# Single-row fetches of a graph kernel: one 1,024-byte piece per row, or sixteen 64-byte pieces, at other rates per queue

## What is computed

```python
w_ij  = silu(ef1 @ W1r + b1r) @ W2r + b2r + silu(ef2 @ W1s + b1s) @ W2s + b2s   # per edge, 128 values
q_i   = (x @ Wq)[dst]; k_j = (x @ Wk)[src]; v_j = (x @ Wv)[src]                 # gathered per edge
alpha = (q_i * w_ij * k_j).sum over each head of 16, / 4, * edge_weight          # 8 heads
out   = segment_sum(alpha * v_j, dst) / 16
y     = layernorm(x + out)
```

## Time and profile before

| | |
|---|---|
| median of 3 runs | 3112.95 us |
| lowest, highest | 3109.12 us, 3114.18 us |
| span of the profiled execution, first to last instruction | 1968.8 us |
| what lies around the span (median less span) | 1144.2 us |
| PE busy | 1721.6 us, 87% of the span |
| VectorE busy | 1571.4 us, 80% |
| GpSimd busy | 1486.6 us, 76% |
| ScalarE busy | 580.1 us, 29% |

### The profile page before, as it was taken

The page is one execution under the profiler, slowest core; times in us unless marked ns, Lnnn a source line. Parts: engine busy times, 40 slices in busy tenths (PEclk is TensorE's granted clock), DMA queues, the critical chain, the costliest instruction groups (busy, mean ns, idle before and its releaser), DMA issues.

```text
span 1968.8 us, 57037 instructions
## 1 busy us (share of the span) xinstructions
PE 1721.6 (87%) x14511; PEld 1255.5 (64%) x14511; DVE 1571.4 (80%) x4327; ACT 580.1 (29%) x1031; POOL 1486.6 (76%) x1568
## 2 busy tenths in 40 slices
PE   8799999999998988888888888888888888888898
PEld 7566666666666666666666656666656565656666
DVE  5588888888887887787777878778777778777887
ACT  5332233333322322232222322222222222222223
POOL 7777777777777777777777777777777777777777
PEclk9899999999998999899888999899999989998988
DMA  9866656666666556555555555555556555565654
GB/s 340 257 173 173 176 173 175 174 175 169 168 169 172 162 167 174 153 172 163 166 154 171 164 166 170 156 173 155 173 156 172 161 166 167 162 172 156 174 154 116
DMA packets 191285, 339.03 MB, mean 172 GB/s; under 512 B 83101, under 2 KB 101262, under 8 KB 190958
## 3 DMA queue, kind: packets, MB, share of 16 engines
q0 software_dynamic: 74192, 202.08, 35.9%
q1 hardware_dynamic: 107696, 126.28, 21.6%
q10 hardware_dynamic: 9070, 7.02, 1.4%
HBM read 320.25 MB, written 14.95 MB: 170 GB/s over the span
## 4 chain that ended last, share of the span: by engine, by line
POOL 51%; PE 25%; issue 18%; DVE 3%; DMA 2%; DVEq 0%; ACT 0%; ACTq 0%; SPq 0%
POOL kvt L672 51%; PE bank L710 11%; PE bank L687 4%; PE bank L725 2%; PE bank L712 2%; DMA kvt<-kvtab,srcS 2%; PE bank L750 1%; PE bank L315 1%; PE bank L700 1%; DVE t L994 1%; PE bank L441 1%; DVE accT L948 1%; PE bank L429 1%; DMA qtab<-qx 0%; PE bank L419 0%
## 5 line engine op out<-in xcount | busy, mean ns | idle before, releaser
L672 POOL DMA_INDIRECT kvt<-kvtab,srcS x1527 | 1449.2, 949 | 465.9 <-issue 461.0
L796 ACT ACTIVATE hs<-bank,B 128x512 f32<-128x512 f32 x806 | 509.4, 683 | 1350.8 <-issue 783.4
L710 PE MATMUL bank<-W2r,hs 128*128 128x128 f32 x3224 | 494.8, 300 | 8.7 <-ACT hs L796 8.7
L994 DVE TENSOR_TENSOR t<-bank,kvt 128x512 f32<-128x512 f32 (+1 forms) x395 | 264.9, 671 | 292.8 <-DMA kvt<-kvtab,srcS 158.0
L710 PEld LDWEIGHTS bank<-W2r,hs 128*128 128x128 f32 x3224 | 419.2, 203 | 86.2 <-issue 71.8
L710 PE MATMUL bank<-W2s,hs 128*128 128x128 f32 x3224 | 453.3, 287 | 0.0
L710 PEld LDWEIGHTS bank<-W2s,hs 128*128 128x128 f32 x3224 | 421.3, 204 | 0.0
L725 PE MATMUL bank<-msg,oh 128*32 128x128 f32 x3216 | 177.4, 292 | 221.5 <-DVE accT L948 218.8
L725 PEld LDWEIGHTS bank<-msg,oh 128*32 128x32 f32 x3216 | 71.7, 109 | 411.8 <-issue 395.9
L1009 DVE TENSOR_REDUCE bank<-t 128x32 f32<-128x512 f32 x402 | 279.3, 695 | 13.8
L687 PE MATMUL bank<-eft,W 32*128 32x512 f32 x1612 | 279.2, 669 | 2.4 <-ACT kvh L481 2.4
(11 more groups left out here) (112 smaller groups left out, 704.5 us busy)
## 6 DMA issues: line engine op xcount, KB each, us to landing
kvA<-kvtab ACTq DMA_DIRECT2D x3968, 1.0 KB
kvS<-kvtab SPq DMA_DIRECT2D x3328, 1.0 KB
eft<-in_ef SPq DMA_DIRECT2D x102, 512.0 KB, 7.4
dbt<-dst SPq DMA_DIRECT2D x102, 384.0 KB, 6.7
kvt<-kvtab,srcS POOLq DMA_INDIRECT x1527
qwt<-qtab SPq DMA_DIRECT2D x403, 24.0 KB
kvtab<-kvt SPq DMA_DIRECT2D x24, 256.0 KB, 7.7
qtab<-qx SPq DMA_DIRECT2D x12, 384.0 KB, 6.4
```

What stands on the lines that cost most here:

```text
L672: pool.indirect_dma_start(kvt[:, (g - HX) % KS, t, :], None, kvtab, bass.IndirectOffsetOnAxis(ap=srcS[:, g * TG + t:g * TG + t + 1], axis= ...
L710: pe.matmul(WB[g % 2][:, t * D:(t + 1) * D], hs[:, g % HS, j, t * 128:(t + 1) * 128], w2[:, :], start=(j == 0 and t == 0), stop=False, ski ...
L796: act.activation(hs[:, g % HS, j, :], HB[i % 4][:, :], ACT.Silu, bias=B1[:, j:j + 1]).then_inc(m_si, 1)
L994: m = dve.tensor_tensor(t1[:, s, a:b, :], tiles(WB[s][:, :])[:, a:b, :], kv[:, :, 0:D], ALU.mult)
```

## The change

Three things change. The rates become 10 rows a group on SyncE and 11 on ScalarE, throughout. A row is written by its DMA not as 1,024 contiguous bytes but as 16 pieces of 64 bytes; piece a of buffer 0 and piece a of buffer 1 lie side by side in the partition, so the pieces of one row are 128 bytes apart. VectorE reads the tile in that layout: a piece is one head of 16 float32 values, 8 pieces are the 128 values of k and the other 8 those of v. The number of DMAs for a row stays one.

```diff
-RS, RA = (8, 9, 272), (10, 10, 0)
+RS, RA = (10, 10, 0), (11, 11, 0)
+PIECES = 16
...
-        kvS = sb("kvS", [128, 2, 2 * D], f32)
-        kvA = sb("kvA", [128, 2, 2 * D], f32)
+        kvS = sb("kvS", [128, PIECES, 2, 2 * D // PIECES], f32)
+        kvA = sb("kvA", [128, PIECES, 2, 2 * D // PIECES], f32)
...
-                return kv_bytes[bass.ds(start_of(reg, (N - 1) * KVROW), KVROW)].rearrange("(o f) -> o f", o=1)
+                return kv_bytes[bass.ds(start_of(reg, (N - 1) * KVROW), KVROW)].rearrange("(o a f) -> o a f", o=1, a=PIECES)
...
-                        sp.dma_start(kvS[p:p + 1, u % 2, :].bitcast(u8), kv_row(sp_row[r - rows_upto(g // BS * BS, RS)])
+                        sp.dma_start(kvS[p:p + 1, :, u % 2, :].bitcast(u8), kv_row(sp_row[r - rows_upto(g // BS * BS, RS)])
...
-                        act.dma_start(kvA[p:p + 1, u % 2, :].bitcast(u8), kv_row(act_row[r - rows_upto(g // BA * BA, RA)])
+                        act.dma_start(kvA[p:p + 1, :, u % 2, :].bitcast(u8), kv_row(act_row[r - rows_upto(g // BA * BA, RA)])
...
+            def heads(t):
+                return t.rearrange("p (h d) -> p h d", h=H)
+
+            def row_tile(g, k):
+                buffer, u = (kvS, use_s[g] % 2) if g in use_s else (kvA, use_a[g] % 2)
+                half = buffer[:, k * PIECES // 2:(k + 1) * PIECES // 2, u, :]
+                return half if PIECES == 2 * H else half.rearrange("p a (h d) -> p (a h) d", d=HD)
...
-                for a, b, kv in kv_parts(g):
-                    m = dve.tensor_tensor(t1[:, s, a:b, :], tiles(WB[s][:, :])[:, a:b, :], kv[:, :, 0:D], ALU.mult)
+                n = gathered(g)
+                m = dve.tensor_tensor(t1[:, s, 0:n, :], tiles(WB[s][:, :])[:, 0:n, :], kv_rows(g)[:, 0:n, 0:D], ALU.mult)
+                if n == KT:
+                    m = dve.tensor_tensor(heads(t1[:, s, KT, :]), heads(tiles(WB[s][:, :])[:, KT, :]), row_tile(g, 0),
+                                          ALU.mult)
...
+                if n == KT:
+                    m = dve.tensor_tensor(heads(msg[:, g % MS, KT, :]), row_tile(g, 1),
+                                          cut_alpha(g)[:, KT * H:TG * H].rearrange("p (h a) -> p h a", a=1)
+                                          .broadcast_to([128, H, HD]), ALU.mult)
```

More of the change, by code:

```diff
@@ L1025, in gnn_program @@
                 dve.wait_ge(m_al, g + 1)
[L1026 to L1030, removed]
+                m = dve.tensor_tensor(msg[:, g % MS, 0:n, :].rearrange("p t (h d) -> p t h d", h=H),
+                                      kv_rows(g)[:, 0:n, D:2 * D].rearrange("p t (h d) -> p t h d", h=H),
+                                      cut_alpha(g)[:, 0:n * H].rearrange("p (t h a) -> p t h a", h=H, a=1)
+                                      .broadcast_to([128, n, H, HD]), ALU.mult)
+                if n == KT:
+                    m = dve.tensor_tensor(heads(msg[:, g % MS, KT, :]), row_tile(g, 1),
+                                          cut_alpha(g)[:, KT * H:TG * H].rearrange("p (h a) -> p h a", a=1)
+                                          .broadcast_to([128, H, HD]), ALU.mult)
                 m.then_inc(m_msg, 1)
```

## The result

The changed kernel takes 4216.9 us (median of 4 runs, 4214.5 to 4224.0), the kernel before 3113.6 us beside it (4 runs, 3109.1 to 3125.0). The ratio is 1.356, 95% interval 1.352 to 1.359: 1103 us slower, where 452 us were forecast.

What follows compares the result with a forecast made beforehand. GpSimd's gathers bound the kernel, ScalarE's queue right under; dearer rows make that queue last at 5.81 us a group, 2420.8 us, +452 us on the span: 3565 us. Forecast's own range 3500 to 3810, 8-in-10 range 3100 to 3810.

Steps and rivals of the forecast that it cites:

- What bounds the kernel: GpSimd's gathers set the late pace, 4.84 us a group; ScalarE's queue at 4.35 us and PE lie right under.
- Fewer gathers: On GpSimd, 8 gathers go at 1.254 us each: 10.0 us less, if nothing else comes last.
- Rows at the old price: On ScalarE's queue, two more rows and a larger register load: 4.78 us a group, span 2012.9 us.
- The sum: Run time from ScalarE's queue: start, 396 groups with rows, 7 without, and end; 5.81 us a group gives 2420.8 us.
- The price of a row in sixteen pieces: On either queue, a row's issue costs what qwt's does, 322 ns, +94 ns; ends 307 and 423 ns.
- What lies around the span: Time outside the profiled span stays as it is, so +452 us on 1968.8 us becomes 3565 us from 3112.95.
- The DMA engines, VectorE's layout: Engines 62% used by some 20 ns a packet, no bound; VectorE's strided reading costs nothing, at most 36 us, hidden.
- rival 4: On the DMA engines, 266,000 packets at 49 ns each take 815 us an engine, gathers land late; no separate chance.
- The signs to look for: In the profile after: row issues of 322 and 329 ns, 69 SiLUs in 200 us, PE under 75% busy.
- Rival 1: On both queues, a row's issue stays 228/235 ns: 3157 us, +44; chance 0.15 for price unchanged or partly raised.
- Rival 2: On the queues, a row's issue gets cheaper, 12 ns less is enough, GpSimd stays last: 3103 us; chance 0.15.
- Rival 3: On the queues, the destination's further dimension costs as with eft, 423 ns: 4006 us; chance 0.05 for over 3850 us.

Runs made afterwards that it cites:

- rows_long_issue: Kernel before, one-piece rows at old rates, with the short way of issuing switched off for SyncE's and ScalarE's rows: 3144.7 us beside 1969.9, ratio 1.596.

## Why the prediction was wrong

- **What bounds the kernel: right, and closer than thought.** GpSimd has the largest part of the chain in the repeat of the kernel before (44% is L672), ScalarE's queue lies right under it. That SyncE's lies as close (231.4 us of waits in 1970) was not said.
- **Fewer gathers, 10 us:** 1,519 gathers as forecast; the gain never showed, as forecast for the case that another resource is last.
- **Rows at the old price: right for ScalarE, wrong for SyncE.** The sum gave a span of 2012.9 us; ScalarE at 11 alone measured 2038.4 and 2056.9, 1.3 and 2.2% more. For SyncE the prediction's list of four groups, at the old price of a row (22.4 less 40 x 0.094), is 18.6 us, 4.66 a group. The run with SyncE at 10 had (2058.6 - 72.6 - 47.4) / 396 = 4.90, 5% more. The price of a row was right, 228 ns, with a mean of 233; the 0.9 us by which four groups are longer lie in small terms. The means instead of the medians of the rows make 0.2 us of it; the load of the query addresses takes 0.57 us in the mean and not 0.3; the stores, 0.19 us, are left out of the list; and dbt and eft take 0.46 and 0.50 us in the mean and not 0.32 and 0.42. On the two together the rates cost 201 us and not 44.
- **The price of a row in sixteen pieces: this step failed.** It put the row with the other DMAs, as "16 pieces belong with 10 and 96", and took qwt's 322 ns, +94. It is 540 ns, +310. Neither end of the range, 307 and 423 ns, held it, because all the rows it was bounded by the earlier trace rows are DMAs on the short way of issuing: with the switch off every one of them rises, the single ones too, out from 307 to 900 ns and b2w from 247 to 748. The trace of before shows no other kind; the price doesn't follow how many pieces there are. What shape loses the mark wasn't mapped: two or more pieces within the one partition that a row goes to lose it, while eft and qtab, with two pieces in each of 128 partitions, keep it. The sentence "From 10 to 96 pieces hardly anything changes" was true and didn't bear on it.
- **The sum: right in form.** With +307 ns instead of +94, two groups are 9.56 + 22 x 0.307 = 16.31 us, 8.16 a group, and the span 72.6 + 396 x 8.16 + 30.5 + 16.9 = 3351 us, 2.7% under the 3444.5 measured. Means serve better than medians here, since some issues are much longer than the median: from row to row it is 0.679 us in the mean and was 0.342. With that +0.337, two groups are 9.56 + 22 x 0.337 = 16.97 us, 8.49 a group, and the span is 3481 us, 1.1% over. The prediction's rule that start-to-start is the duration + 90 ns nearly held: the gap between two rows is 98 ns in the mean.
- **What lies around the span: a wrong assumption.** The 1144 us between a median from one session and a span from another are no constant to be added. Where a profiled run has both, they differ by 1.7 us. So the 1144 us in the table of before don't lie outside of the instructions of one execution. With the right price the same addition would have given 3351 + 1144 = 4495 us, 7% over the 4216.9 measured: in the session of the timed runs the change costs 1103 us, in the other kind 1485 us, and the prediction had no term for the difference.
- **The DMA engines, VectorE's layout: hidden, as forecast.** Queue 10 has 140,398 packets against the forecast 140,000, at 2.1 to 2.6% of the engines' time, 10 ns a packet in the mean where some 20 were taken. That also rules out rival 4: the DMA engines' share fell, from 0.57 and more to 0.29 and 0.30 in the stretches above, 0.36 and 0.37 in the repeat. VectorE's multiply of a row tile takes 281 ns in the new layout and 280 before, so the stride costs nothing. rows_long_issue, which leaves VectorE as it was, takes the same time within 0.3%.
- **The signs to look for.** "Issue" before nearly all SiLUs: 341 waits of 2417 us in all, yes. 69 SiLUs in 200 us: 47 in the repeat, by the pace of its 95 in 400 us, and 39 in the timed session, so both slower than forecast. PE under 75%: 76% and 57%. The granted clock, a mean over the run of its two levels of 1.2 and 2.4 GHz, went from 0.95 to 0.72 of the higher one, as PE's busy share fell; with 4% of the chain PE doesn't end the run.
- **The rivals.** Rival 1, the price unchanged, would have been 2171 us beside 1970. Rival 2, a cheaper issue, has nothing for it. Rival 3 had the right direction, a dearer issue for the further dimension, at a chance of 0.05.

## What to carry to other kernels

The duration of an issue on a queue isn't a property of size alone: a DMA that lays down one row as two or more pieces in one partition can leave the short way of issuing, and then costs 540 to 645 ns where 228 was paid, on the queue that issues it. When a change gives a transfer a shape that no transfer of the trace has, bound its price by a row that shares the shape's new feature, and if there is none, say that the upper end is open; the other DMAs of the kernel aren't a bound. And if the profiled span and the median time of the runs lie far apart, they are of two conditions, and the difference is no constant to add.

## What the runs showed of the hardware that was not expected

- A row issue takes 228 ns for one piece, 630 to 645 for 2, 4 and 8, and 544 for 16. So two to eight pieces are dearer than sixteen.
- Without the mark contiguous rows, then cut by the builder, take 540 ns as well, and qwt, dbt and eft rise by 215, 266 and 265 ns.
- Among long rows on the same queue the other DMAs, unchanged in the source, get longer too; why was not tested. qwt in the repeat of the changed kernel (322/322/458 in the earlier trace rows):

```profile
L609 SPq DMA_DIRECT2D qwt<-qtab x403: 317/526/1782, 71.8 to 3415.7; - x135
```

- The same program took 3105 us and 1972 us on one chip in two sessions, so the chip alone doesn't decide it. In the timed session of the changed kernel a register move of SyncE, 29 ns and at most 38 in the repeat, takes up to 1890 ns (both rows stand above), GpSimd's longest pause without a releaser is 20.5 us and not 0.3, and the waits whose releaser the profile gives as another core or an unknown queue are 2275 us, summed over the engines, where the repeat has none. What causes them wasn't found.
- None of these kernels beats the kernel before. Its rates stand where GpSimd and both queues end nearly together: taking 3 gathers from GpSimd (1,524 after 1,527) costs 78 us by way of ScalarE's queue, and taking 5 costs 89 us by way of SyncE's.
